# The layers' order: from fixed due times to a plan by readiness and rank

## The reference

```python
# B, N, D = 4, 1024, 256
xn = layernorm(x)                        # no scale, no shift
s = attention(xn)                        # 16 heads of 64, causal, keys and values from a latent of 64
f = xn
for l in range(2):                       # DEPTH
    h = shift_token(f)                   # second half of the channels comes from the token before
    q, k, v = split(h @ wqkv[l])         # 8 heads of 64
    q, k = l2norm(q) * qs, l2norm(k) * ks; q, k = rotary_xpos(q, k)
    f = f + local_attention(q, k, v) @ wo[l]          # window 128: own block and the one before, causal
    h = layernorm(shift_token(f)) * lg + lb
    a, g = split(h @ w1[l] + b1[l])      # 682 each
    f = f + (a * gelu(g)) @ w2[l] + b2[l]
out = x + s * silu(f)
```

## Time and profile before

| | |
|---|---|
| median of 3 runs | 2378.74 us (2377.64 to 2388.44) |
| profiled execution, its own time | 2376.21 us |
| its span, first to last instruction | 2374.4 us |
| mean granted TensorE clock | 0.933 |
| TensorE busy | 2068.5 us, 87% |
| VectorE busy | 1713.8 us, 72% |
| GpSimd busy | 1435.8 us, 60% |
| ScalarE busy | 1307.7 us, 55% |

### The profile page before, as it was taken

One profiled execution on the slowest core, in us unless ns is written; L12 is line 12 of the kernel. 1 busy time (PEld: TensorE's weight loads), 2 busy tenths in 40 slices (PEclk: granted clock), 3 DMA queues, 4 the chain that ended last, 5 costly groups with the idle time before them and its releaser, 6 DMA issues. The chain is left out here.

```text
span 2374.4 us, 44883 instructions
## 1 busy us (share of the span) xinstructions
PE 2068.5 (87%) x15232; PEld 1616.4 (68%) x15232; DVE 1713.8 (72%) x3132; ACT 1307.7 (55%) x3178; POOL 1435.8 (60%) x1209
## 2 busy tenths in 40 slices
PE   6579999999899899999998789798889978888875
PEld 4467777777677677777776566576667756676654
DVE  5587776777767887677774378787777777878773
ACT  2356666766566566765673464545544555455541
POOL 2465666656665666556662167766767676758673
PEclk7789999999999999999999789999989999999988
DMA  8343333333333433333323137776768676867685
GB/s 270 97 100 87 91 94 91 79 90 89 95 79 90 113 94 86 75 91 85 91 72 95 43 90 179 181 179 153 179 158 196 148 182 168 204 146 188 163 192 121
DMA packets 191583, 298.16 MB, mean 126 GB/s; under 512 B 52265, under 2 KB 97661, under 8 KB 190333
## 3 DMA queue, kind: packets, MB, share of 16 engines
q1 hardware_dynamic: 179068, 271.17, 45.4%
q10 hardware_dynamic: 12288, 24.13, 4.2%
HBM read 56.04 MB, written 20.97 MB: 32 GB/s over the span
## 5 line engine op out<-in xcount | busy, mean ns | idle before, releaser
L1966 POOL TENSOR_TENSOR g_pt<-g_pt,g_rl 128x1024 f32<-128x1024 f32 (+2 forms) x112 | 293.2, 2625 | 123.3 <-DVE g_rl L1902 119.2
L1689 PE MATMUL ps<-g_turned,g_latV 128*64 128x256 f32 (+1 forms) x1984 | 303.0, 451 | 64.7 <-issue 47.3
L851 ACT ACTIVATE l_pp<-ps,l_mx 128x256 f32<-128x256 f32 (+1 forms) x512 | 228.4, 463 | 167.9 <-DVE l_mx L988 167.8
L1790 ACT ACTIVATE g_pt<-ps,g_mx 128x256 f32<-128x256 f32 (+3 forms) x256 | 200.9, 796 | 166.9 <-DVE g_mx L1884 79.8
L1966 POOL TENSOR_TENSOR g_pp<-g_pp,g_rl 128x768 f32<-128x768 f32 (+3 forms) x112 | 238.4, 2137 | 83.6 <-DVE g_rl L1902 83.3
L1127 POOL TENSOR_TENSOR l_pp<-l_pp,l_rl 128x1024 f32<-128x1024 f32 (+1 forms) x128 | 229.7, 1795 | 87.4 <-DVE l_rl L996 87.4
L1790 ACT ACTIVATE g_pp<-ps,g_mx 128x128 f32<-128x128 f32 (+3 forms) x256 | 173.3, 690 | 166.6 <-DVE g_mx L1884 69.9
L1689 PEld LDWEIGHTS ps<-g_turned,g_latV 128*64 128x64 f32 x1984 | 147.2, 147 | 153.8 <-issue 88.0
L1665 PE MATMUL ps<-g_lat_hi,g_q_hi 64*128 64x256 f32 (+3 forms) x896 | 182.1, 394 | 73.5 <-ACT g_pp L1790 33.4
L1914 DVE STREAM_TRANSPOSE g_bt<-g_pt 128x1024 f32<-128x1024 f32 (+1 forms) x176 | 194.2, 1127 | 67.8 <-DMA g_turned<-g_bt 47.7
L1144 POOL TENSOR_TENSOR l_act_lo<-l_u,l_act_hi 114x512 fp32r<-114x512 f32 x96 | 125.4, 1307 | 158.1 <-ACT l_act_hi L901 157.9
(11 more groups left out here) (191 smaller groups left out, 6023.8 us busy)
## 6 DMA issues: line engine op xcount, KB each, us to landing
l_pt<-l_bt SPq DMA_DIRECT2D x1024, 64.0 KB, 2.0
g_turned<-g_bt SPq DMA_DIRECT2D x320, 128.0 KB, 3.1
g_turned<-g_bt SPq DMA_DIRECT2D x320, 96.0 KB, 2.4
g_turned<-g_bt SPq DMA_DIRECT2D x224, 112.0 KB, 2.8
g_turned<-g_bt SPq DMA_DIRECT2D x224, 80.0 KB, 2.1
l_tab<-turns SPq DMA_DIRECT2D x64, 128.0 KB, 2.1
g_turned<-g_bt ACTq DMA_DIRECT2D x64, 128.0 KB, 3.9
g_turned<-g_bt SPq DMA_DIRECT2D x96, 64.0 KB, 2.0
```

What stands on the lines that cost most here:

```text
L851: act.activation(PP[:, i % NP, at, 0:n], ps[:, bank + a, jj * 2 * P:jj * 2 * P + n], ACT.Exp, bias=mx[:, g % 2, h, at:at + 1], scale=-1.0, ...
L1689: last = pe.matmul(o, latV[:, b % 2, c, :], turned[:, :, a, c, :, :], start=(c == 0), stop=(c == t), skip_group_check=True)
L1790: act.activation(probs(k, a), scored(k, a)[0], ACT.Exp, bias=mx[:, u % 2, at:at + 1], accum_out=sm[:, u % 2, at:at + 1]).then_inc(s["ex"], 1)
L1966: pool.tensor_tensor(view, view, rl[:, u % 2, mine(k):mine(k) + n].unsqueeze(2).to_broadcast([P, n, keys(u)]), ALU.mult).then_inc(s["scale ...
```

## The change

`Flow` no longer sorts by due times. Its events stand in one queue for each kind and engine, in their natural order, and `Order.arrange`, moved out of `Plan` unchanged, interleaves them. It keeps a clock for each engine, takes the engine with the earliest clock, and among the heads of its queues whose needs (`needs`: data, buffers, and for TensorE free PSUM banks) are met in the model picks the one with the lowest `rank`; if none is ready, the engine's clock goes on to the next time at which one is. `cost` gives the model's duration from the table `TOOK`, 1.3 more where ScalarE changes its function table. The ranks have the form of the old due times, with many of the constants changed. `room` and `claim` choose banks by when the model has them free, two-bank events on odd pairs too. The instructions inside the events are unchanged, and so are `Plan`'s costs, ranks and banks; nothing else in the kernel changes.

```diff
-class Flow:
+class Order:
+    def arrange(self):
...
+class Flow(Order):
     PIECES, FIRST = 12, 4
+    NV, NA = 5, 3
-    DUE = {
+    RANK = {
         "sp": {
-            "bring": (...), "load": -33.45, "xload": -24.37, "store": -20.4, "move": -29.2},
+              "bring": (...),
+              "load": -29.3, "xload": -20.43, "store": -25.69, "move": -29.2},
-            "proj": -3.66, "val": -3.55, "turn": -2.22, "scores": (-1.88, -1.86), "weigh": 0.45, "wo": 4.61,
-            "mean": 5.08, "var": 5.31, "centre": 5.44, "up": (5.8, 5.92, 6.16, 6.59, 6.6, 7.04),
-            "down": (6.61, 7.05, 7.37, 7.82, 7.87, 8.09)},
+        "pe": {"proj": -3.66, "val": -3.55, "turn": -8.2, "scores": (-5.21, -1.86), "weigh": 0.45, "wo": 4.61,
+              "mean": 5.08, "var": 5.41, "centre": 5.44, "up": (5.8, 5.92, 6.72, 6.59, 6.6, 7.04),
+              "down": (6.59, 7.03, 7.35, 7.8, 7.85, 8.07)},
-            "split": -3.96, "proj": -3.23, "norm": -2.43, "val": -2.47, "turn": -1.76, "divide": 1.05, "mean": 5.63,
-            "var": 5.68, "centre": 5.89, "up": (6.24, 6.53, 6.74, 6.99, 7.05, 7.38),
-            "gate": (6.43, 6.63, 7.04, 7.18, 7.73, 8.04), "scores": (-1.28, -1.05)},
+        "act": {"split": -3.58, "proj": -19.72, "norm": -2.43, "val": -2.06, "turn": -3.18, "divide": 1.05,
+              "mean": 5.63, "var": 5.68, "centre": 5.89, "up": (6.8, 6.53, 6.74, 6.99, 7.05, 7.38),
+              "gate": (6.43, 6.63, 7.04, 7.18, 7.73, 8.04), "scores": (-4.58, -1.05)},
...
+              "scores": (-1.3, -1.26), "proj": -3.03, "turn": 1.19, "wo": -1.01, "mean": 8.98, "centre": 5.92,
+              "up": (6.38, 6.54, 7.41, 7.06, 7.26, 7.66), "out": 8.55, "share": (-1.37, -1.04),
+              "blocks": (-0.51, -0.87), "divide": 1.32, "low": 5.98},
+        "pool": {"split": -12.23, "norm": -8.44, "var": -2.68, "gate": (-2.44, -1.97, -1.53, -0.81, -1.23, -0.63),
+              "scale": (-8.89, -8.53)},
+    TOOK = {"pe": {"proj": 2.8, "val": 1.4, "turn": 1.0, "scores": 0.85, "weigh": 1.95, "wo": 5.6, "mean": 2.1, "var": 1.9,
+                   "centre": 0.6, "up": 2.8, "down": 1.4},
+            "act": {"split": 0.35, "proj": 0.95, "norm": 0.6, "val": 0.5, "turn": 0.95, "scores": 1.8, "divide": 0.5, "mean": 1.0,
+                    "var": 0.95, "centre": 1.25, "up": 0.6, "gate": 0.55},
+            "dve": {"bring": 1.5, "proj": 3.8, "turn": 1.15, "scores": 1.55, "share": 0.15, "blocks": 1.15, "divide": 0.62,
+                    "wo": 1.25, "mean": 1.25, "centre": 1.35, "low": 1.35, "up": 0.68, "out": 1.35},
+            "pool": {"split": 0.72, "norm": 5.1, "scale": 1.9, "var": 0.65, "gate": 1.25},
+            "sp": {"load": 1.6, "bring": 0.7, "move": 9.4, "xload": 0.6, "store": 0.6}}
+    LANDING = {"load": 2.6, "bring": 4.5, "xload": 4.5, "store": 3.6, "move": 2.4}
+    SWITCH = 1.3
...
-        self.program = {engine: self.events(engine) for engine in self.DUE}
-        self.place()
+        self.queues = {engine: {kind: self.events(engine, kind) for kind in kinds} for engine, kinds in self.RANK.items()}
+        self.gelu = False
+        self.arrange()
...
+        late = 0.2 if engine == "act" and self.gelu and kind in ("scores", "norm", "var") else 0.0
+        return at + late + (n if kind in self.TILES else TC * n)
...
+    def cost(self, engine, event):
+        kind, n = event[:2]
+        took = self.TOOK[engine][kind]
+        if kind in ("scores", "blocks", "scale", "weigh") and n % NT == 0:
+            took *= 0.6
+        if engine == "act" and kind in ("up", "scores", "norm", "var"):
+            if self.gelu != (kind == "up"):
+                took += self.SWITCH
+            self.gelu = kind == "up"
...
+    def room(self, event, free, now):
+        n = self.BANKS[event[0]][0]
+        runs = [range(i, i + n) for i in range(9 - n) if all(free[k] is not None for k in range(i, i + n))]
+        if n == 1:
+            alone = lambda i: sum(0 <= k < 8 and (free[k] is None or free[k] > now) for k in (i - 1, i + 1)) + (i in (0, 7))
+            return (min((r[0] for r in runs), key=lambda i: (max(now, free[i]), -alone(i), i)),) if runs else None
+        return tuple(min(runs, key=lambda r: (max(now, free[r[0]], free[r[1]]), r[0] % 2, r[0]))) if runs else None
...
-class Plan:
+class Plan(Order):
```

More of the change, by code:

```diff
@@ new lines, in rank, with events @@
+        return at + late + (n if kind in self.TILES else TC * n)
+    def events(self, engine, kind):
+        at = self.RANK[engine][kind]
+        if kind == "bring":
+            return [(kind, n) for n in range(self.FIRST, DEPTH * self.PIECES)]
+        some = [(kind, n) for n in range(self.T if kind in self.TILES else self.Q)]
+        return [e + (i,) for e in some for i in range(len(at))] if isinstance(at, (tuple, list)) else some
+    def cost(self, engine, event):
[7 more added lines that the diff above has]
+            self.gelu = kind == "up"
+            if kind == "up" and event[2] in (2, 5):
+                took += self.SWITCH
+                self.gelu = False
+        return took
@@ new lines, in claim @@
+    def claim(self, event, banks, free, holder, until):
+        kind, n = event[:2]
+        if not banks:
+            self.bank[event], self.before[event] = self.bank[kind, n, 0], []
+            return
+        self.bank[event] = banks[0]
+        self.before[event] = list(dict.fromkeys(holder[i] for i in banks if holder[i]))
+        _, engine, name = self.BANKS[kind]
+        reader = (engine, (name, n) if kind == "down" else (name,) + event[1:])
+        for i in banks:
+            free[i], holder[i] = None, event
+            until.setdefault(reader, []).append(i)
@@ L1382, in needs @@
         return out
[L1384 to L1417, removed]
-            _, kind, event, banks = best
-            at[engine][kind] += 1
-            left -= 1
-            self.program[engine].append(event)
-            took = self.cost(engine, event)
-            for other, since in waiting.items():
-                if clock[other] is not None:
-                    clock[other] = min(clock[other], max(since, now))
-            waiting = {}
-            clock[engine] = now + took
-            done[engine, event] = now + took + (0.2 if engine == "pe" else self.LANDING.get(kind, 0.1) if engine == "sp" or
-                                                kind == "move" else 0.1)
-            for i in until.pop((engine, event), ()):
-                free[i] = done[engine, event]
-            if engine == "pe":
-                self.claim(event, banks, free, holder, until)
-        self.span = max(done.values())
@@ L1436, in ready, with stays @@
-    def ready(self, engine, event, done, free, wanted, now):
-        times, banks = [0.0], ()
-        for need in wanted[engine, event]:
-            if need not in done:
-                return None, ()
-            times.append(done[need])
-        if engine == "pe" and not (event[0] in ("weigh", "wout") and event[2]):
-            banks = self.room(event, free, now)
-            if banks is None:
-                return None, ()
-            times += [free[i] for i in banks]
-        return max(times), banks
+    def stays(self, event):
+        return event[0] in ("weigh", "wout") and event[2] > 0
```

200 lines of the change are left out of this document (175 added, 25 removed).

## The result

| | before | after |
|---|---|---|
| median | 2377.44 us (16 runs, 2365.97 to 2388.44) | 2396.58 us (16 runs, 2386.75 to 2409.43) |
| profiled execution | 2376.2 us, clock 0.933 | 2389.8 us, clock 0.937 |

The ratio is 1.0088, with a 95% interval of 1.0072 to 1.0104. The change is slower by 21 us. I had forecast 2348 us. The time lies within my range of 2306 to 2398 us, near its upper end, but I had called a gain the likeliest and it is a loss.

What follows compares the result with a forecast made beforehand. TensorE was taken to bound the layers, with only its idle time and clock winnable. Steady stretch 22 plus fill 8 made 30 us less than 2376.2, 2346; with the median's 2.5 us offset 2348.7, stated as 2348, range 2306 to 2398.

Steps and rivals of the forecast that it cites:

- Steady stretch: Layers' repeating chunks: list scheduling wins half the idle time, 1.6 us a chunk, 22 us over 14; ends -67 and +45.
- those four places: TensorE waits: "up" for "low", transposes for exps' banks, scores for low half, variance matmuls for squares; 3.2 us a chunk.
- The clock: Steady stretch: full-size matmuls behind narrow variance matmuls run at 1.2 GHz, 1.6 us a chunk; no gain taken.
- Fill: 75 to 192.5 us: projection fills TensorE's waits before scores, 8 us less taken; ends -22 and +5.
- a sign of being wrong: In the profile after: TensorE waits for norms, weighed blocks or moved tiles that have no row today.
- Change of layer: New layer's projection: underpriced weight pieces put it 4.6 us early in the plan; 0 taken, ends -4 and +5.
- End: After the last tile only the last chunk's chain is left, no other work to place there; 0.
- ScalarE's tables: Norm's Ln after a Gelu: two table loads, model charges one 1.3 us switch; delay inside the steady stretch's bounds.
- Sync queue: Tile moves: model prices 9.4 us, chip took 10.8, so weighing comes about 1.4 us late; inside steady stretch's bounds.
- readiness without slack: Rival 2: late norms delay transposes, scores, exps; banks held longer; 5 us of new waits a chunk, +27 us, 2406; chance 0.16.
- More and smaller gaps, lower clock: Rival 3: spread gaps bring the low clock twice more a chunk, +48 us, 2427 us; chance 0.06.

## Why the prediction was wrong

*Steady stretch*: the failed step. It was "TensorE gets other work in those four places" and the half of 3.2 us a chunk that I took for it, -22 us. The stretch from the first to the last "mean" grew by 26.6 us instead (1111.0 to 1137.6 by their start rows, cut as above), with 17.4 us more of idle time in it. The distances between the starts of "mean", in us, show where; the second column is the run with GpSimd writes, which has the old order and the time of the kernel before, and so tells how far two traces differ by themselves:

| | before | same order, with writes | change | change, norms kept off "low" |
|---|---|---|---|---|
| first to second | 72.8 | 76.0 | 82.7 | 85.7 |
| seventh to ninth (change of layer) | 153.2 | 154.8 | 164.6 | 162.5 |
| the other eleven chunks | 831.2 | 833.0 | 833.8 | 823.5 |
| last but one to last | 53.7 | 56.6 | 56.5 | 56.3 |

In the eleven chunks I had counted on 18 us less, and nothing was won. Three of the four places did get other work there, and the blocking and the small new waits took it back: with the norms kept off "low" these chunks do gain some 0.7 to 0.9 us each, by these single traces. Most of the loss lies in the first two lines, 7 to 11 us in each. My sum held the second at nothing and counted the first among the undisturbed chunks. The rows for them and for the last distance, before:

```profile
192.46:265.30 72.84, 69.62 (x470) 55.11 (x469) 56.61 (x129) 48.44 (x117) 45.15 (x46) 1.00 0.33 83
...
648.21:722.67 74.46, 71.21 (x469) 56.24 (x469) 53.31 (x125) 48.40 (x117) 44.93 (x46) 0.98 0.36 91
722.67:801.39 78.72, 72.36 (x485) 57.16 (x485) 67.04 (x135) 50.63 (x120) 49.86 (x47) 0.98 0.37 95
...
1249.71:1303.44 53.73, 45.13 (x277) 35.35 (x277) 23.05 (x43) 21.11 (x41) 12.26 (x12) 0.94 0.31 79
```

and the change:

```profile
188.20:270.90 82.70, 76.25 (x541) 60.36 (x539) 64.60 (x144) 53.54 (x132) 54.43 (x56) 1.00 0.39 96
...
653.49:731.91 78.42, 73.37 (x457) 58.61 (x456) 57.08 (x114) 47.37 (x113) 48.17 (x51) 0.96 0.32 83
731.91:818.09 86.18, 76.08 (x510) 59.24 (x511) 75.45 (x159) 52.43 (x133) 51.57 (x50) 0.97 0.38 99
...
1269.32:1325.78 56.46, 45.87 (x220) 35.17 (x221) 15.24 (x21) 17.57 (x26) 12.27 (x12) 0.81 0.21 56
```

The plan does some 70 matmuls more than the old order between the first and the second "mean". It has 57 fewer left for the last distance, and that one gets no shorter, so the work done early isn't paid back at the end.

I took for granted that an order from a planner's model is a better one on the chip. It isn't, since the model lacks the overlaps inside events (they are worth 37 us to the old order and 16 to 22 to the new one), and the blocking (15 us). I had listed the model's wrong durations, which can be read off the rows beside `TOOK`; corrected, they won nothing. What the model leaves out altogether I didn't look for. The overlaps were there to be read, in the code's semaphores and in any row of a Gelu; the blocking was not, since the old order all but avoids it: its longest half of a "low" takes 1.04 us (the row is in the last section).

The plan that knows the overlaps wins 1.8 us a chunk in its steady stretch, near the 1.6 that I took, but that is luck: 0.8 us of it is idle time, where I took 1.6, and most of the rest is the clock, where I took nothing.

*The clock* (0): right in number, not in mechanism. I took it that the level would go on falling behind the variance matmuls. In the kernel before it falls there in ten chunks. In the change it falls directly behind them in none; it falls behind gaps instead, mostly the long one ahead of "up". I added up, from the first "mean" to the last and without the gaps, by how much the matmuls of 512 columns start further apart than 0.23 us: 45 us before, 53 in the change, and 54 in the run with GpSimd writes, whose time is that of the kernel before. So the clock has no part in the loss that goes beyond the difference between two traces of the old order.

*Fill*: taken as -8, and no gain is shown. The first "mean" came at 188.2 us, not before 185, and the old order reaches it as early in other traces (188.5 us in the run with writes). The scores' wait for the low half fell from 25.2 us, but only to 11.0 (the longest 4.1 us, where I had said none above 3), and new waits of the transposes for the norm came up, which I had named as a sign of being wrong; TensorE's waits from 75 to 188 us, beside the earlier trace rows:

```profile
PE ps L891 <- POOL l_t L1328: 12.7, 3, 6.9
PE ps L909 <- DVE l_qk_lo L1179: 11.0, 4, 4.1
```

*Change of layer* (taken as 0): the chunk in which the layer changes, from the eighth "mean" to the ninth, took 86.2 us against 78.7, 7.5 us more, beyond my upper end of 5, and the one ahead of it 3.9 us more. Waits on late weights, for which I had set the +5, are not among TensorE's waits there. *End* (0): from the last "mean" to the last store nothing changed (44 us in both). *ScalarE's tables* and *Sync queue*: they are in the corrected prices, which won nothing.

Of the rivals, *readiness without slack* (2406 us) came nearest in sign and size, but not by its mechanism: prices were not it, and the new wait stands at "up" and not at the transposes. *More and smaller gaps, lower clock* has no part in it that can be told from chance: the mean clock of the stretch is 0.96 against 0.97, and the sum above is as large in a run of the old order. Its argument against itself, that the gap of 1.4 us ahead of "up" doesn't bring the lower level, rested on one chunk; two of fifteen do the opposite.

Open: why the replay is 16 us too hopeful for the plan with overlaps, and what makes the first distance and the change of layer longer under every plan that was run (83 to 90 us and 162 to 178 us, where the old order takes 73 to 77 and 153 to 161). No run took the early work, the blocking and the new waits at these places apart.

## What to carry to other kernels

A planner's model is only as good as the cases in which it ranks two orders as the chip does: replay the old order in it before trusting the new one, and look at the ends and at each change of phase and not only at the steady stretch. Here it called an order 62 us better that was 21 us worse. Look for what the model lacks in kind (starts inside an event, shared paths) before its durations, and refit the constants to the loop that uses them. Give short work on the critical path a neighbour engine that doesn't read SBUF just then.

## What the hardware showed that I had not expected

One GpSimd instruction of 1.9 us in the wrong place stopped a VectorE instruction of 0.74 us for 1.6 us more, and was itself slowed from 1.90 to 2.23 us. The halves of "low" in the change (ns: shortest, median, longest), and before:

```profile
L1254 DVE SCALAR_TENSOR_TENSOR l_h_lo<-l_u,l_lb,l_h_hi x32: 721/784/2384, 206.4 to 1341.1; 128x512 fp32r<-128x512 f32 x32
```

```profile
L1045 DVE SCALAR_TENSOR_TENSOR l_h_lo<-l_u,l_lb,l_h_hi x32: 736/741/1037, 207.4 to 1317.9; 128x512 fp32r<-128x512 f32 x32
```

The same work beside a GpSimd that only writes kept its time. And gaps of 1.0 to 1.4 us ahead of "up" were followed by the clock's lower level in two of fifteen chunks of the kernel before, the change's nine gaps of 3.3 to 5.6 us in all nine.
